# A gated cross-attention block: chunks 1 to 7 of x fetched already turned, with new orders on every engine

## The reference

```python
x = x + jnp.tanh(g_xattn[0]) * _L0_xattn_ref(_layernorm(x, axis=-1), ctx_1024, ctx_1024, ...)
x = x + jnp.tanh(g_ffn[0]) * _L0_ffn_ref(_layernorm(x, axis=-1), L0_ffn_w1, L0_ffn_b1, L0_ffn_w2, L0_ffn_b2)
```

## Time and profile before

| what | before |
|---|---|
| median of 3 runs | 622.41 us (622.37 to 625.25) |
| span of the profiled execution | 619.4 us |
| PE busy | 584.2 us, 94% of the span |
| DVE busy | 480.4 us, 78% |
| ACT busy | 328.0 us, 53% |
| POOL busy | 202.9 us, 33% |
| attention block, about | 0 to 371 us |
| hidden block, about | 371 to 490 us |
| output block, about | 490 to 619 us |

### The profile page before, as it was taken

How to read it: one execution, slowest core, us unless ns; L and a number is a source line. 1 busy time by engine, 2 the same in 40 slices (tenths; PEclk the granted TensorE clock), 3 DMA queues, 4 the chain that set the end, 5 groups by cost and what they waited for, 6 DMA issues and landing times. The chain is left out here.

```text
span 619.4 us, 9745 instructions
## 1 busy us (share of the span) xinstructions
PE 584.2 (94%) x3415; PEld 339.3 (55%) x3415; DVE 480.4 (78%) x690; ACT 328.0 (53%) x395; POOL 202.9 (33%) x175
## 2 busy tenths in 40 slices
PE   6999899999998999999989788999999989999997
PEld 5845657557566566575675475444444454444443
DVE  6968889978889788688675785989999788965361
ACT  2444365751743725527327236777776669544440
POOL 3125153632431712424108230000001809803473
PEclk9999899999999999999999999999999999999999
DMA  9922000460100100001001119877776969889753
GB/s 311 404 72 93 1 1 2 137 204 0 69 2 0 69 1 31 40 0 68 0 1 68 69 68 324 305 281 294 275 271 251 425 232 348 321 310 386 251 218 141
DMA packets 37188, 98.20 MB, mean 159 GB/s; under 512 B 2720, under 2 KB 3488, under 8 KB 32544
## 3 DMA queue, kind: packets, MB, share of 16 engines
q1 hardware_dynamic: 35808, 96.36, 41.5%
q10 hardware_dynamic: 1344, 1.37, 0.7%
HBM read 55.77 MB, written 41.94 MB: 158 GB/s over the span
## 5 line engine op out<-in xcount | busy, mean ns | idle before, releaser
L1233 PE MATMUL ps<-h_sb,w_q 128*128 (+1 forms) x488 | 109.6, 379 | 1.8 <-ACT xo L1295 1.8
L1497 PE MATMUL ps<-w_q,h_q 128*128 128x512 bf16 x448 | 96.9, 379 | 0.0
L1031 POOL TENSOR_TENSOR c_lo<-c_sb,c_hi 128x512 fp32r<-128x512 f32 x32 | 41.4, 1302 | 111.3 <-ACT c_hi L588 111.3
L1233 PEld LDWEIGHTS ps<-h_sb,w_q 128*128 128x128 bf16 x488 | 46.8, 98 | 53.8 <-ACT xo L1295 2.4
L1579 POOL TENSOR_TENSOR xo<-xo,b2s 128x512 f32<-128x512 f32 x32 | 56.4, 1795 | 60.5 <-DMA xo<-x_dram 42.0
L1497 PEld LDWEIGHTS ps<-w_q,h_q 128*128 128x128 bf16 x448 | 43.8, 98 | 52.9
L1295 ACT ACTIVATE xo<-ps,b1s,sc 128x1024 f32<-128x1024 f32 x48 | 57.6, 1204 | 20.0 <-PE ps L1233 19.0
L575 ACT ACTIVATE prob<-ps 77x1024 f32<-77x1024 f32 x64 | 61.6, 1012 | 7.7 <-PE ps L385 7.7
L1366 DVE TENSOR_REDUCE hmax<-xo 128x1024 f32 (+1 forms) x48 | 57.0, 1212 | 9.7 <-ACT xo L1295 9.7
L623 ACT ACTIVATE q_hi<-ps,bq_sb 128x512 fp32r<-128x512 f32 x32 | 22.0, 687 | 78.0 <-PE ps L343 77.9
L1040 POOL TENSOR_TENSOR x<-x,bo_gate 128x512 f32<-128x512 f32 (+1 forms) x32 | 41.5, 1310 | 49.3 <-DVE xn L742 33.4
(11 more groups left out here) (147 smaller groups left out, 1100.3 us busy)
## 6 DMA issues: line engine op xcount, KB each, us to landing
h_dram<-xo SPq DMA_DIRECT2D x48, 512.0 KB, 2.7
h_sb<-h_dram SPq DMA_DIRECT2D x16, 1024.0 KB, 11.0
x_dram<-x SPq DMA_DIRECT2D x8, 1024.0 KB, 3.9
xo<-x_dram SPq DMA_DIRECT2D x8, 1024.0 KB, 4.8
x<-h_dram SPq DMA_DIRECT2D x8, 1024.0 KB, 7.8
x<-in_x SPq DMA_DIRECT2D x7, 1024.0 KB, 5.5
out<-xo SPq DMA_DIRECT2D x7, 1024.0 KB, 4.4
x<-in_w_t SPq DMA_DIRECT2D x1, 4096.0 KB, 20.2
```

The costliest lines, as they stand in the source:

```text
L1031: nc.gpsimd.tensor_tensor(c_lo[:, g, :], c_sb[:, g, :], c_hi[:, g, :].bitcast(F32), ALU.subtract).then_inc(c_lo_on, 1)
L1233: mm = nc.tensor.matmul(ps[:, 2 * (m % 2) + s, :], w1_q[:, k, m * P:(m + 1) * P], xq_t[:, one(2 * j + s), k, :], start=(k == 0), stop=(k = ...
L1497: mm = nc.tensor.matmul(ps[:, 4 * s + t, :], h_q[s][:, m, t * P:(t + 1) * P], w2_q[:, m, :], start=(m == 0), stop=(m == MF - 1))
```

## The change

The host passes x a second time, turned (`x_t`, 512 x 4096). For chunks 1 to 7 the kernel no longer normalizes and turns x on the chip; chunk 0 is prepared as before.

- `load_xt(n, k)`: SP fetches quarter k of chunk n, 128 features by 512 tokens, 256 KB, into one of two buffers `xr`.
- `pass_rstd(c)`: 1/deviation of a chunk's 512 tokens is written to DRAM as single values and read back into a row of 512 that all partitions hold (`row`). SP waits for the write before it issues the read.
- `scale_xt`: POOL multiplies a quarter by the row. ACT copies the high part (`xt_high`), POOL subtracts the low part (`xt_low`), both from SBUF.
- The mean is taken off by centred weights: `weight_means` is 8 matmuls in step 0, ACT copies the means, POOL subtracts them from the four quarters of Wq, ACT makes `wq_hi` and POOL `wq_lo` anew. Step 1 waits for that.
- All engines have new orders, in functions `first_step`, `step(i)` and `last_steps`, without hardware loops. `project_out(c, t, begin, end)` can be issued in pieces. Results of `project_out` use banks `W0` and `W1` in turn, and the last chunk's high and low parts go to `xt_hi` and `xt_lo`.
- The second padding memset of `prob` goes; `group_ones` has zeros in its place. The bf16 copy of the identity is made by POOL at the start of `hidden`.

The diff, cut to the functions that matter here:

```diff
+                def load_xt(n, k):
+                    if n == 1 and k < 2:
+                        sp.wait_ge(xt_mm, TT)
+                    elif k < 2:
+                        sp.wait_ge(xt_lo_on, KD * (n - 1) + k + 3)
+                    else:
+                        sp.wait_ge(xt_lo_on, KD * n + k - 1)
+                    sp.dma_start(xr[:, k % 2, :], xt_v[k, n]).then_inc(xr_in[k % 2], 16)
+
+                def pass_rstd(c):
+                    sp.wait_ge(ln1_rstd, rstd_value(c))
+                    sp.dma_start(sh.rstd_dram[c].rearrange("(t p) -> p t", p=P), rstd1[:],
+                                 allow_slow_non_contiguous=True).then_inc(row_out, 16)
+                    sp.wait_ge(row_out, 16 * c)
+                    if c >= 2:
+                        sp.wait_ge(xr_mul, KD * (c - 1))
+                    sp.dma_start(row[:], as_row(sh.rstd_dram[c]).to_broadcast([P, CH])).then_inc(row_in, 16)
...
+                for i in range(1, NC):
+                    n = i + 1
+                    if n < NC:
+                        load_xt(n, 0)
+                        load_xt(n, 1)
+                        if i == 2:
+                            load_x(W1_T // TT)
+                        load_xt(n, 2)
+                        load_xt(n, 3)
+                    if i == 2:
+                        for c in range(W1_T // TT + 1, NC):
+                            load_x(c)
+                    if i >= 2:
+                        store_x1(i - 2)
+                    if n + 1 < NC:
+                        pass_rstd(n + 1)
+                store_x1(LAST - 1)
+                store_x1(LAST)
...
+                def weight_means():
+
+                    pe.wait_ge(w_lo_on, KD)
+                    pe.wait_ge(idents_on, 5)
+                    terms = [(w, k) for w in (wq_hi, wq_lo) for k in range(KD)]
+                    for j, (w, k) in enumerate(terms):
+                        mm = nc.tensor.matmul(ps[:, BC, :], sh.pick[:, GROUPS:GROUPS + 1].to_broadcast([P, P]),
+                                              w[:, k, :], start=(j == 0), stop=(j == len(terms) - 1))
+                    mm.then_inc(wmean_mm, 1)
...
+                        if m == 0 and w is wq_hi and r is xt_hi:
+                            if c == 0:
+                                pe.wait_ge(w_hi_on, k + 1)
+                            else:
+                                pe.wait_ge(xt_lo_on, KD * c + k + 1)
...
+                        pe.wait_ge(q_lo_on, KD * i + 3)
+                        project_out(i - 2, 2, 0, 7)
                     scores_by_token(i, 3)
-                    if first:
-                        project_v(1, range(KD // 2))
-                    if prev2:
-                        project_out(i - 2, 2, BS)
+                    if older:
+                        project_out(i - 2, 2, 7, ALL)
+                        pe.wait_ge(q_lo_on, KD * i + KD)
+                        project_out(i - 2, 3, 0, 2)
                     transpose_max(i)
...
+                    if older:
+                        project_out(i - 2, 3, 2, ALL)
+                    else:
                         idle_turns(nc, sh, W1, 16)
...
+                    values(i, 0)
+                    sums(i, 0)
+                    if older:
+                        pe.wait_ge(x1_on, TT * (i - 2) + 3)
+                    project_out(i - 1, 0, 0, 3)
+                    project_out(i - 1, 0, 3, ALL)
                     scores_by_key(i, 3)
+                    project_out(i - 1, 1, 0, 6 if i == LAST else ALL)
+                    values(i, 2)
+                    sums(i, 2)
...
+                def last_steps():
+                    values(LAST, GROUPS - 1)
+                    sums(LAST, GROUPS - 1)
+                    project_out(LAST - 1, 1, 6, ALL)
+                    pe.wait_ge(x1_on, TT * (LAST - 1) + 1)
+                    project_out(LAST - 1, 2, 0, ALL)
+                    pe.wait_ge(c_on, GROUPS * NC)
+                    project_out(LAST - 1, 3, 0, ALL)
...
+                def xt_high(n, k):
+                    act.wait_ge(q_mm, KD * n)
+                    act.wait_ge(xr_mul, xr_count(n, k))
+                    nc.scalar.copy(xt_hi[:, k, :], xr[:, k % 2, :]).then_inc(xt_hi_on, 1)
...
+                        if m == 1:
+                            act.wait_ge(wmean_mm, 1)
+                            nc.scalar.activation(wq_mean[:], ps[:, BC, :], ACT.Copy,
+                                                 scale=1.0 / D).then_inc(wmean_on, 1)
...
+                    if nxt:
+                        xt_high(n, 0)
+                        xt_high(n, 1)
+                    max_row(i)
+                    exponentials(i, 0)
+                    exponentials(i, 1)
...
+                    divide(i - 1, 0)
+                    token_max(i, 1)
+                    q_low(i, 2)
+                    token_max(i, 2)
+                    q_low(i, 3)
+                    token_max(i, 3)
+                    divide(i - 1, 1)
...
+                    residual(i - 1, 0)
+                    stats2(i - 1, 0)
+                    if i == 1:
+                        w1_scale()
+                    if i < LAST:
+                        residual(i - 1, 1)
                         stats2(i - 1, 1)
+                    amax2(i - 1, 0)
+
+                def last_steps():
+                    reciprocals(LAST)
+                    divide(LAST, 0)
+                    residual(LAST - 1, 1)
+                    divide(LAST, 1)
+                    divide(LAST, 2)
+                    residual(LAST - 1, 2)
+                    divide(LAST, 3)
+                    residual(LAST - 1, 3)
+                    for t in range(1, TT):
+                        stats2(LAST - 1, t)
+                    for t in range(1, TT):
+                        amax2(LAST - 1, t)
...
+                def scale_xt(n, k):
+
+                    pool.wait_ge(xr_in[k % 2], xr_value(n, k))
+                    pool.wait_ge(row_in, 16 * n)
+                    xa = xr[:, k % 2, :]
+                    nc.gpsimd.tensor_tensor(xa, xa, row[:], ALU.mult).then_inc(xr_mul, 1)
+
+                def xt_low(n, k):
+                    pool.wait_ge(xt_hi_on, KD * n + k + 1)
+                    nc.gpsimd.tensor_tensor(xt_lo[:, k, :], xr[:, k % 2, :], xt_hi[:, k, :].bitcast(F32),
+                                            ALU.subtract).then_inc(xt_lo_on, 1)
...
+                def first_step():
+                    pool.wait_ge(k_biased, GROUPS)
+                    nc.gpsimd.tensor_copy(sh.k_t1[:], k_t[:, :, NK:B * NK]).then_inc(k_kept, 1)
+                    rstd_1(1)
+                    pool.wait_ge(w_lo_on, KD)
+                    pool.wait_ge(wmean_on, 1)
+                    for k in range(KD):
+                        nc.gpsimd.tensor_tensor(wq_raw[:, k, :], wq_raw[:, k, :], wq_mean[:],
+                                                ALU.subtract).then_inc(wc_on, 1)
+                    scale_xt(1, 0)
+                    scale_xt(1, 1)
+                    for k in range(KD):
+                        pool.wait_ge(wc_hi_on, k + 1)
+                        nc.gpsimd.tensor_tensor(wq_lo[:, k, :], wq_raw[:, k, :], wq_hi[:, k, :].bitcast(F32),
+                                                ALU.subtract).then_inc(wc_lo_on, 1)
+                    xt_low(1, 0)
+                    xt_low(1, 1)
+                    for t in range(TT):
+                        add_bias(0, t)
+                    scale_xt(1, 2)
+                    scale_xt(1, 3)
+                    xt_low(1, 2)
+                    xt_low(1, 3)
+                    for t in range(TT):
+                        add_bias(1, t)
+                    rstd_1(2)
...
+                    if i == 2:
                         for k in range(KD):
                             if k == 0:
                                 pool.wait_ge(w_lo_on, 2 * KD)
                             pool.wait_ge(w1_rounded, k + 1)
                             nc.gpsimd.tensor_scalar(sh.w1_i8[:, k, :], w1_raw[:, k, :], -MAGIC, 1.0, ALU.add,
                                                     ALU.mult).then_inc(w1_narrow, 1)
-                    if is_step(i, 0):
-                        pool.wait_ge(bog_on, 1)
+                    if nxt and i >= 2:
...
-                            add_bias(0, t)
+                            add_bias(n, t)
+                    if i in (LAST - 2, LAST - 1):
+                        normalize2(i - (LAST - 2))
                     if nxt:
...
+                        xt_low(n, 0)
+                        xt_low(n, 1)
+                        scale_xt(n, 2)
+                        scale_xt(n, 3)
...
+                    for g in range(GROUPS):
+                        c_low(i - 1, g)
+                    if i >= 2:
+                        rstd_2(i - 2)
+                    if nxt:
+                        xt_low(n, 2)
+                        xt_low(n, 3)
+                    if i == 1:
+                        for t in range(TT):
```

(4 more changed lines are left out.)

843 lines of the change are left out of this document (403 added, 440 removed).

## The result

The changed kernel takes **662.95 us** (median of 4 runs, 662.25 to 664.78) where the kernel before takes 622.64 us in the same series. The ratio is 1.0632, 95% interval 1.0606 to 1.0658: the change is **6.3% slower**. The forecast was 609.0 us, the range 601 to 617. The profiled execution has a span of 662.6 us.

What follows compares the result with a forecast made beforehand. The prediction took PE to be the bound, busy 40.0 of 41.4 us in step 3. Its terms summed to -13.4 us, from a span of 619.4 to 606.0, plus 3.0 for the median: 609.0 us, range 601 to 617.

Steps and rivals of the forecast that it cites:

- term 6: Row and quarters in the other steps: P, the row's way through DRAM, taken as 7 us, costed at nothing.
- the cover: In the other steps: `xt_low` can begin only at 15.5 us, POOL works to 11.8, so 3.7 us are spare.
- the row holds everything up: Rival: a late row holds POOL, period P + 24.9 us, kernel slower, 640 us at P = 18.2; chance 0.08.
- term 1: Turns removed from PE: 28 groups at 0.53 us, -14.8 us, bounds -12.3 to -17.6.
- term 2: Steps 2 to 6: matmuls fill PE's waits for DVE's maxima, with 0.1 us of room, and `xt_low` waits shrink: -7.0 us.
- Term 4: Step 0 and the start of step 1: `weight_means` +1.4 us, POOL's queue +1.5 us, the latter with bounds 0 and 4.
- Term 5: Step 2: PE waits for the first `c_low` of chunk 1 behind POOL's queue, +6.6 us, bounds 0 and 9.
- terms 3 and 7: Shorter waits in step 7, -3.0 us; a later DVE end in the last chunk, +0.9 us.
- term 8: Clock after the first block: PE pauses nearly 4 us at the end, +1.0 us, bounds 0 and 3.
- The reading by which term 8 would be 0: End of first block: transposes don't count for the clock gate, today's pause was as long, sum 1.0 us lower.

Runs made afterwards that it cites:

- e2: The changed kernel with 1/deviation written as 128 pieces of 16 bytes instead of 512 single values (tokens get each other's scales): 623.46 us.
- e3: The changed kernel with a copy in place of the maximum of w1 over partitions, which is left out: 661.71 us.
- b1: The kernel before with only seven of twelve `project_out` matmuls moved between the third and fourth token scores: 624.33 us, ratio 1.0005.
- e7: The changed kernel with 16-byte pieces (tokens get each other's scales) and a copy instead of the maximum of w1 over partitions: 616.54 us.
- e13: The changed kernel, whole computation: 16-byte pieces, renamed tokens, maximum without POOL, reordered POOL and x loads, `values` and `sums` written by tiles: 609.55 us, ratio 0.9774.
- e16: The changed kernel with 512 single values written 64 bytes apart in DRAM and the row read from `bo` (scales left out): 622.80 us.
- e9: The changed kernel with 16-byte pieces, renamed tokens, and ACT and POOL reading c with a stride to keep weight loads dense: 625.65 us.
- e6: The changed kernel with 16-byte pieces made right by renaming tokens; the last projection takes each fourth column as weights: 631.41 us.

## Why the prediction was wrong

**The step that failed is term 6**, the way of the row. It said "by two landings of 2.3 us, 4.6, below, and two of 9.1 us, 18.2, above", and "so I take 7, near the lower end". In the sum the term stood at nothing, and e2 says that the slow store costs 39.5 us. The measured 14.8 to 17.6 (15.0 in e3 for the chunk that has 19.4) lie at the upper end, which I set aside because its rows stood in full queues. The lightly used queues told nothing: the store takes 8.5 us by itself. The bounds held these and the choice between them was wrong, and the nearest row by size was the 9.1 us of the 0.5 KB gate, not the load of a 64 KB identity. With 16-byte pieces P is 6.9 us and PE waits for neither `c_low` nor `xt_low` in steps 3 to 6 (e2): the 7 and the cover were right, but for a store that the kernel does not make.

**The rival "the row holds everything up" is what happened**, with a chance of 0.08. Its formula, a period of P + 24.9, can be seen: where nothing else is in the queue, POOL's chain from the first scaling to the end of `rstd_1` is 25.8 us (224.8 to 250.6), and with 15.2 the next scaling comes 40.9 us after the last. But it priced P = 15 at 621 us, and the estimate of P near 46 us in the same rival is far off on the other side. Three things were missing. The chain is longer where POOL has more to do: 35.0 us in step 2 (the narrowing; the standstill at the reduce lies ahead of it, in the 19.4 of P), 30.7 in step 5, where POOL's own normalizing of the second kind stands (4.0 us with its first row, above), which my list of POOL's work did not have. Waits reach PE through ACT's queue in steps 0 and 1 (6.70 and 5.90 us). And the clock is lower around the waits, which adds some 14 us to PE's busy time.

The other terms, read from e2, where the row is fast:
- **Terms 1 and 2**, 3.5 us a middle step, in parts of 2.1 and 1.4: measured 3.0 (41.4 to 38.4). By PE's busy time in a middle step (39.9 us before, 38.4 now) the turns gave 1.5 of it, a little under the low bound of term 1 (4 x 0.44, 1.8), and the waits the other 1.5. b1 shows that the 7.0 us of term 2 are worth nothing by themselves; its waits for `xt_lo` and the maxima say that DVE has no room as long as it makes `xt_low` and the normalized tiles. My words "with little to spare" were right and the sum ignored them.
- **Term 4**, the first step: 0.8 us later in sum at the first score of step 1, measured 0.7 in e2. In the changed kernel it is 10.5, far over the bound of 4: P is 15.7 us in step 0, where the term had the row in 6.8 us after `rstd_1`.
- **Term 5**, 6.6 us for `c_low` in step 2: measured 6.97, and 7.05 without the reduce (e7). But the step takes 47.8 us, not 44.5, for the most part because the clock is lower behind the wait: PE is busy 40.5 us in it, for 38.4 in step 3.
- **Missing altogether**: `partition_all_reduce`. The rows of POOL in e2:

```profile
94.64 1.02 POOL L1100 TENSOR_TENSOR rstd<-ve,minus_half 128x4 f32<-128x4 f32 x1
102.51 0.38 POOL L1221 PARTITION_ALL_REDUCE wmax<-wmax  x1 [6.84 <-DMA row<-rstd_dram]
109.74 2.55 POOL L1107 TENSOR_TENSOR xr<-xr,row 128x512 f32<-128x512 f32 x2 [6.85 <-ACT x L713]
```

  It runs 0.38 us with 6.8 us of standstill on each side. In the kernel before the same call had such gaps, but POOL was needed by nobody there. The change puts it on POOL's way and puts DVE's `w1_scale` ahead of a residual that PE waits for: DVE stands still 13.3 us for its result in e2. e7 says that it costs 6.9 us. The Trainium skill ("GPSIMD Engine Reference", Instruction dispatch) says that the first call of a freshly loaded kernel pays about 6 us for loading code, with no instruction to be seen. The trace agrees with a gap of such a length ahead of the call, 6.8 us here and 5.7 to 9.2 in the other runs, and has one behind the call too; no run shows what fills either.
- **Terms 3, 7 and 8**: from the last step to the start of `hidden` e2 takes 58.9 us for 61.5 before, 2.6 less, where terms 3 and 7 said 2.1 less. The pause of 3.86 us at the end was there, as forecast. The granted clock is 0.50 behind it, from 373 to 375 us, and what follows the first block takes 250.2 us for 248.6 before, 1.6 more, where term 8 said 1.0. The reading by which term 8 would be 0 did not come.

So the first block of e2 ends at 371.1 us where the terms put 356.4 (370.8 less 14.4, since the 1.0 of term 8 falls behind it): 9.1 us more in step 1 (47.9 for 38.8, which is 40.9 less the turns; 6.9 of it are the reduce), 3.3 in step 2, 2.8 in steps 3 to 6 together, and 0.5 less at the end.

That e13 takes 609.55 us and the forecast says 609.0 is in part a coincidence. Its first block ends at 356.9, but step 2 takes 40.9 us for the 44.5 of the forecast, since the narrowing has moved, and about as much is lost again by a later start (1.5) and by longer steps: 1.7 in step 1 and 1.7 in steps 3 to 6 together.

## What to carry to other kernels

A value that crosses partitions through DRAM should not be stored as single values that are 4-byte neighbours; look at the row of a store of the same layout before taking a price from a load. When work moves to a quiet engine, list all that this engine does in each step, what stands on it for several microseconds, and what is queued behind the waits on the engines that copy for it: a late value holds up everything in order behind its first reader. And a wait before an instruction is worth removing only if the engine that ends it has room; otherwise it comes back one instruction later.

## What the runs showed of the hardware

- Stores of single 4-byte values side by side in DRAM land in 7.8 to 8.5 us, whether 128 or 512 of them; 512 values 64 bytes apart in 2.0 (e16), and 128 pieces of 16 bytes in 1.4 (e2).
- A stride of 16 bytes in SBUF costs ACT's copy 1093 ns for 623 and POOL's subtraction 1539 for 1329 (e9, e2), and a weight load 311 for 187 (e6, e2). The Trainium skill ("SBUF — State Buffer", Door 1: The DMA port swizzle) speaks of lines of 16 bytes, with a penalty for each access to a new one; these runs agree.
- The same section says that any access to PSUM that isn't contiguous slows matmuls down much. In e13 `values` writes rows whose neighbouring tokens are 512 bytes apart, and its matmuls take 604 ns in the mean, against 612 in e2, and step 5 takes 38.4 us in e13 and 38.5 in e2: the measurement decides, for this layout.
- A standstill of PE of 5.9 us was followed by 4 us at a granted clock of 0.50. Over steps 0 to 6 the lower clock of the changed kernel came to some 14 us, by the difference in busy time above.
